# Cross-attention block with a two-expert feed-forward net: weight chunks split from step 8, row ranks in three parts, the first routed tile gathered earlier, two blocks normalised in the setup

## What is computed

```python
def block(x, context, ...):
    x = x + xattn(layernorm(x), context)          # 16 heads of 64, 64 keys
    z = layernorm(x)
    one_hot = argmax(softmax(z @ gate_w.T))       # 2 experts
    masked = z[None] * one_hot.T[:, :, None]      # a row not chosen enters as zeros
    routed = sum_e(relu(masked[e] @ w1[e] + b1[e]) @ w2[e] + b2[e])
    shared = relu(z @ sw1 + sb1) @ sw2 + sb2
    return x + routed + shared                    # hidden size 2048
```

## Time and profile before

| | before |
|---|---|
| time, median of 3 runs | 1908.87 us (1908.34 to 1910.06) |
| the profiled execution | 1907.19 us, span 1905.5 us |
| PE busy | 1826.0 us (96% of the span) |
| DVE, ACT, POOL busy | 798.1, 820.3, 509.2 us |
| mean granted clock of PE | 0.986 of full speed |
| bytes moved | 214.44 MB, mean 113 GB/s |

### The profile page before, as it was taken

The page is one execution under the profiler, slowest core; times in us unless marked ns, Lnnn a source line. Parts: engine busy times, 40 slices in busy tenths (PEclk is TensorE's granted clock), DMA queues, the critical chain, the costliest instruction groups (busy, mean ns, idle before and its releaser), DMA issues.

```text
span 1905.5 us, 33426 instructions
## 1 busy us (share of the span) xinstructions
PE 1826.0 (96%) x11516; PEld 1149.4 (60%) x11517; DVE 798.1 (42%) x1649; ACT 820.3 (43%) x1441; POOL 509.2 (27%) x477
## 2 busy tenths in 40 slices
PE   8979999999799999999999998999999999999997
PEld 6335444544466666666666665666666666666664
DVE  6967778777244433342333333222222222222222
ACT  3645555554333334334444443333333333433333
POOL 2047777776101111221100001122221112122111
PEclk9989999999899999999999999899999999999998
DMA  9235555555942333223344493822121111212100
GB/s 322 83 86 147 161 166 166 175 157 150 267 110 78 100 95 94 90 86 121 121 121 136 151 302 114 247 56 56 51 62 45 38 44 47 60 44 61 51 24 15
DMA packets 230151, 214.44 MB, mean 113 GB/s; under 512 B 130864, under 2 KB 172336, under 8 KB 229680
## 3 DMA queue, kind: packets, MB, share of 16 engines
q1 hardware_dynamic: 221120, 188.09, 34.2%
q0 software_dynamic: 8944, 25.19, 4.3%
HBM read 129.57 MB, written 59.02 MB: 99 GB/s over the span
## 4 chain that ended last, share of the span: by engine, by line
PE 67%; DMA 1%; DVE 1%; issue 1%; ACT 1%; SPq 1%; POOL 0%; POOLq 0%; ACTq 0%
PE pH L998 34%; PE pY L1010 33%; DMA e_split<-s_el 1%; DVE s_el L1341 1%; ACT room_a L1023 0%; ACT s_eh L1255 0%; DVE room_a L1029 0%; SPq L1146 0%; ACT room_a L1021 0%; DMA room_a<-rows_room 0%; SPq L1147 0%; POOL rows_room L1409 0%; DVE room_a L1037 0%; DVE s_work L1296 0%; SPq L980 0%
## 5 line engine op out<-in xcount | busy, mean ns | idle before, releaser
L998 PE MATMUL pH<-room_a,room_w 128*128 128x256 f16 (+1 forms) x6336 | 770.8, 272 | 29.4 <-DMA room_a<-rows_room 10.3
L1010 PE MATMUL pY<-room_w,room_a 128*128 128x512 f16 (+1 forms) x3120 | 755.2, 380 | 6.1 <-DVE room_a L1029 6.1
L998 PEld LDWEIGHTS pH<-room_a,room_w 128*128 (+1 forms) x6336 | 613.1, 98 | 215.6 <-issue 33.3
L1029 DVE TENSOR_TENSOR room_a<-room_a 128x256 f16<-128x256 f32 (+1 forms) x528 | 237.6, 450 | 900.9 <-ACT room_a L1023 900.8
L1010 PEld LDWEIGHTS pY<-room_w,room_a 128*128 128x128 f16 x3120 | 304.7, 98 | 270.0 <-DVE room_a L1029 7.1
L1021 ACT ACTIVATE room_a<-pH,e_bsel,sc 128x256 f32<-128x256 f32 (+1 forms) x272 | 151.7, 558 | 432.9 <-PE pH L998 408.1
L1021 ACT ACTIVATE room_a<-pH,b1s,sc 128x256 f32<-128x256 f32 x256 | 144.1, 563 | 360.1 <-PE pH L998 360.1
L1205 POOL TENSOR_TENSOR room_a<-room_a,s_brow 128x512 f32<-128x512 f32 x32 | 42.4, 1344 | 543.6 <-DVE room_a L1037 543.6
L470 PE MATMUL pO<-room_w,room_b 128*128 (+1 forms) x768 | 172.7, 382 | 4.8 <-DVE room_b L682 4.8
L1023 ACT ACTIVATE room_a<-pH,e_bsel,sc 128x256 f16<-128x256 f32 (+1 forms) x272 | 149.5, 550 | 0.0
L1023 ACT ACTIVATE room_a<-pH,b1s,sc 128x256 f16<-128x256 f32 x256 | 142.4, 556 | 0.0
(11 more groups left out here) (175 smaller groups left out, 1341.7 us busy)
## 6 DMA issues: line engine op xcount, KB each, us to landing
s_er<-in_w SPq DMA_DIRECT2D x64, 512.0 KB, 5.0
room_w<-e_split SPq DMA_DIRECT2D x8, 2048.0 KB, 18.6
rows_room<-in_x SPq DMA_DIRECT2D x32, 256.0 KB, 3.0
room_a<-in_sw SPq DMA_DIRECT2D x32, 256.0 KB, 4.2
room_b<-in_x SPq DMA_DIRECT2D x32, 256.0 KB, 3.7
s_split<-room_a SPq DMA_DIRECT2D x64, 128.0 KB, 3.8
x_scratch<-room_b SPq DMA_DIRECT2D x32, 256.0 KB, 4.0
z_split<-room_b SPq DMA_DIRECT2D x32, 256.0 KB, 4.1
```

Source lines behind the costliest of these rows:

```text
L998: mm = q.matmul(self.pH[j % 2][:, 0:rows], w[:, k, j * P:(j + 1) * P], zt[:, u, k, 0:rows], start=(n == 0), stop=(n == 3 * KC - 1))
L1010: mm = q.matmul(self.pY[u][r][:, :], h[:, j % self.HR, r * P:(r + 1) * P], w[:, j, :], start=(j == 0 and n == 0), stop=(j == HC - 1 and n ...
L1029: q.tensor_tensor(self.hl[:, j % self.HR, 0:rows], self.hf[:, j % self.HR, 0:rows], self.hh[:, j % self.HR, 0:rows], ALU.subtract).then_in ...
```

## The change

1. `AT` becomes `(8, 13)`: the first chunk of each shared tile is handled at steps 8 to 10 and no longer at 10 to 12. This holds for the looking in tiles 0 to 7 as well as for the splitting in tiles 8 to 15.
2. `slots` is cut into `row_ranks` (13 instructions, after step 4 of tile 1), `tile_experts` (8, after step 7) and `row_slots` (9, after step 10).
3. `by_tiles` and the picking of routed tile 0 move from step 13 of tile 15 to step 12 of tile 14; POOL gathers before the bias of tile 14; SP transposes before it stores the last chunk. Result, bias and store of shared tile 15 move behind the barrier, into the experts' block: DVE takes the result after `lo_h` of step 1 of routed tile 0, POOL adds the bias before its first wait, and SP stores it before `load_set`. The bias row `brow` gets a room that lives through both blocks.
4. Row blocks 0 and 1 are both normalised within the setup: DVE's statistics at i = 13 and 16, ACT's `normal` ahead of products `NM + 20` and `NM + 23`, and `lo_x` of both on DVE (at i = 23 and 26) instead of POOL.

```diff
@@ block 1 @@
+                def early(g, u, d):
+                    return isinstance(g, int) and 0 <= N * g + u + d <= 1
...
-                            if n == NF - 5:
-                                normal(act, 0, 0)
+                            if n in (NM + 20, NM + 23):
+                                normal(act, 0, (n - NM - 20) // 3)
...
                         deviation(pool, 0, 0)
+                        deviation(pool, 0, 1)
                         pool.wait_ge(s_max, 3)
                         pool.partition_all_reduce(amsr[:, :], ams[:, :], P, RMAX).then_inc(reduced, 1)
                         pool.memset(least, -NEG).then_inc(S["least_set"], 1)
-                        lo_x(pool, 0, 0)
+                        pool.wait_ge(S["xl"], 2)
...
-                            if i == 15:
-                                stats(dve, 0, 0)
-                                stats_done(dve, 0, 0)
-                                aggregate(dve, 0, 0)
-                                add_eps(dve, 0, 0)
-                                shifts(dve, 0, 0)
+                            if i in (13, 16):
+                                stats(dve, 0, (i - 13) // 3)
+                                stats_done(dve, 0, (i - 13) // 3)
+                                aggregate(dve, 0, (i - 13) // 3)
+                                add_eps(dve, 0, (i - 13) // 3)
+                            if i in (15, 18):
+                                shifts(dve, 0, (i - 15) // 3)
+                            if i in (23, 26):
+                                lo_x(dve, 0, (i - 23) // 3)
@@ blocks 2 and 3 @@
+def add_bias(q, g, u, net, brow):
+    q.wait_ge(net.S["o"], net.tile(g, u) + 1)
+    for r in range(net.R):
+        v = q.tensor_tensor(net.ob[:, u, r, :], net.ob[:, u, r, :], brow[:, :], ALU.add)
+    v.then_inc(net.S["ob"], 1)
+
+def store_rows(sp, net, res_d, t):
+    sp.wait_ge(net.S["ob"], t + 1)
+    sp.dma_start(net.rows(res_d, t), net.ob[:, t % net.N, :, :]).then_inc(net.S["out", t % net.N], 16)
...
-        AT = (10, 13)
+        AT = (8, 13)
...
+                sp.wait_ge(S["h"], HC * (TILES - 1))
+                enet.transpose_rows(sp, 0)
                 store_e(2 * TILES - 1)
-                store(TILES - 1)
-                enet.transpose_rows(sp, 0)
...
-                        step(pool, g, u, -1, bias)
+                        if last_tile(g, u):
+                            gather(pool, enet, enet.zb, z_d, iz, 0, 0, enet.S["pick_z"], "rows_in")
+                        if not past(g, u):
+                            step(pool, g, u, -1, add_bias, net, brow)
...
-                            if j == 3:
+                            if j == 3 and not past(g, u):
                                 step(dve, g, u, -1, net.result, 16, 16)
...
-                            if j == 3 and isinstance(g, int) and g == 0 and u == 1:
-                                slots()
-                            if j == 13 and last_tile(g, u):
+                            if isinstance(g, int) and N * g + u == 1 and j in (4, 7, 10):
+                                {4: row_ranks, 7: tile_experts, 10: row_slots}[j]()
+                            if j == 12 and N * g + u == TILES - 2:
                                 by_tiles()
                                 pick_rows(dve, enet, iz, order, 0, 0, enet.S["pick_z"])
...
             def _(sp):
                 sp.dma_start(b2r[:, :, :].rearrange("p e n -> p (e n)"), b2.rearrange("e n -> (e n)").partition_broadcast(P)).then_inc(S["b2_in"], 16)
+                store_rows(sp, snet, res_d, TILES - 1)
                 sp.wait_ge(snet.S["e_out"], 64 * TILES)
...
+                add_bias(pool, TILES // N - 1, 1, snet, brow)
...
                             step(dve, g, u, 0, net.lo_h, j)
+                            if j == 1 and first_tile(g, u, 0):
+                                snet.result(dve, TILES // N - 1, 1, 16, 16)
```

More of the change, by code:

```diff
@@ L334, in last_tile, with lo_x @@
                     return isinstance(g, int) and N * g + u == SUB - 1
+                def early(g, u, d):
+                    return isinstance(g, int) and 0 <= N * g + u + d <= 1
+                def lo_x(e, g, u):
+                    e.wait_ge(S["xn"], count(g, u))
+                    e.tensor_tensor(xs[:, u % 2, DM:2 * DM], xnf[:, u % 2, :], xs[:, u % 2, 0:DM], ALU.subtract).then_inc(S["xl"], 1)
                 def first_tile(g, u, d):
@@ L584, in body @@
                                 step(act, g, u, -1, normal2)
-                                if not first_tile(g, u, 4):
+                                if not early(g, u, 4):
                                     step(act, g, u, 4, normal)
@@ L1126, in load_r @@
                     sp.dma_start(net.rb[:, t % N, :, :], net.rows(x1_d, t)).then_inc(S["r_in", t % N], 16)
-                def store(t):
-                    sp.wait_ge(S["ob"], t + 1)
-                    sp.dma_start(net.rows(res_d, t), net.ob[:, t % N, :, :]).then_inc(S["out", t % N], 16)
                 def load_e(q):
@@ L1175, in _ @@
                     if t > 0:
-                        store(t - 1)
+                        store_rows(sp, net, res_d, t - 1)
                     if t >= PASS:
@@ L1200, in place_rows @@
                                                 bounds_check=SLOTS - 1, oob_is_err=False).then_inc(S["scattered"], 16)
-                def bias(q, g, u):
-                    q.wait_ge(S["o"], net.tile(g, u) + 1)
-                    for r in range(net.R):
-                        v = q.tensor_tensor(net.ob[:, u, r, :], net.ob[:, u, r, :], brow[:, :], ALU.add)
-                    v.then_inc(S["ob"], 1)
                 def body(g):
@@ L1283, in expert_scales, with row_ranks @@
                     assert steps[0] == EXP_STEPS, steps[0]
-                def slots():
-                    link, steps = linker(dve, S["sort"])
+                link_sort, sorted_steps = linker(dve, S["sort"])
+                before, total, run0, run1, slot = (work[:, n, :] for n in range(5))
+                count1, e0_tiles = run1[:, SUB - 1:SUB], work[:, 5, 0:1]
+                def row_ranks():
+                    link, run, other = link_sort, run0, run1
                     dve.wait_ge(S["ranks"], 1)
-                    before, total, run, other, slot = (work[:, n, :] for n in range(5))
                     link(dve.tensor_copy(before, pR[:, 0:SUB]))
@@ L1298, in slots, with tile_experts @@
                         d *= 2
-                    count1, e0_tiles = run[:, SUB - 1:SUB], work[:, 5, 0:1]
+                def tile_experts():
+                    link = link_sort
                     link(dve.tensor_scalar(is1[:, 0:HALF], starts[:, 0:HALF], count1, float(ROWS), ALU.add, ALU.is_ge))
@@ L1309, in slots, with row_slots @@
                     link(dve.tensor_scalar(half_at[:, :], lane[:, 0:SLOT_SUBS], half_sub, None, ALU.is_equal))
+                def row_slots():
+                    link, run, other = link_sort, run1, run0
                     link(dve.tensor_tensor(other, run, total, ALU.subtract))
@@ L1318, in slots @@
                     link(dve.tensor_copy(worki[:, :], slot))
-                    assert steps[0] == SORT_STEPS, steps[0]
+                    assert sorted_steps[0] == SORT_STEPS, sorted_steps[0]
                 def by_tiles():
```

21 lines of the change are left out of this document (8 added, 13 removed).

## The result

The changed kernel took 1880.2 us (median of 4 runs, 1879.3 to 1881.7), the kernel before 1909.4 (1908.3 to 1910.1): ratio 0.985, 95% interval 0.983 to 0.987, or 26 to 32 us less.

A forecast was written before the change was run, and what follows sets the result against it. PE works 96% of the span, so its stops and the slow matmuls behind them count. Terms 11.0 + 5.5 + 8.0 + 4.5 = 29.0 us off the median gave 1880 us; range 1876 to 1889.

The forecast's parts named there:

- case A: Whole kernel: the terms hold as summed, 1880 us, within small errors 1877 to 1884; chance 0.64.
- three signs of being wrong: `lo_x` several microseconds on DVE; PE waiting for a transfer starting routed tile 1; ACT idling over 3.3 us before second chunk.
- Chunks, 11.0: Shared tiles 8 to 15: with the first chunk at step 8, ACT's wait for stores goes, saving 11.0 us.
- the free 3.3 us: Shared tiles 8 to 15: up to 3.3 us of ACT's wait for a store is not felt by PE.
- Case D: Shared tiles: stores issued at step 10 land as late as before, so the chunks' 11.0 us is lost, 1891; chance 0.06.
- Ranks, 5.5: Shared tile 1: three parts remove PE's 3.7 us stop for `lo_h` and 1.8 us of slow matmuls, saving 5.5 us.
- The border, 8.0: Border of blocks 2 and 3: PE starts 8.0 us earlier, plus 0.8 for fewer slow matmuls, less 0.8 waiting.
- I take 0.8: Start of routed tile 1: the cushion of 12 us is used up, so PE waits 0.8 us.
- case C: Routed tile 1 waits: load and transposes need 4 us more, with 1.8 us of slow matmuls, 1886; chance 0.12.
- Case E: Block 3: the store of shared tile 15's result holds up SP's queue, slower than before, 1922 us; chance 0.03.
- Two blocks in the setup, 4.5: End of the setup: `sim` starts right behind the splits and `masked` comes 4.5 us earlier.
- Case B: Setup: DVE is held in `lo_x` until POOL's reduction is over, gain 23.1 us, 1886; chance 0.11.

The follow-up runs named there:

- r1: The changed kernel with the first chunk back at step 10 (`AT = (10, 13)`), the rest kept: 1895.7 us, ratio 0.9933 to the kernel before.
- r3: The changed kernel with the three parts of the ranks in one piece again, at step 3 of shared tile 1: 1885.6 us, ratio 0.9882 to before.
- e5: The changed kernel with the setup of before (one block normalised there, its low part on POOL): 1887.9 us, ratio 0.9894 to before.
- e7: The changed kernel with the low parts of both blocks on POOL in place of DVE, both still normalised in the setup: 1886.9 us, ratio 0.9884 to before.
- e8: The changed kernel with the store of shared tile 15's result moved behind the load of expert 1's weights in SP's queue: 1879.4 us, ratio 0.9850 to before.
- e9: The changed kernel with chunks at steps 7 and 12, and shared tile 15's result stored behind the weight load: 1877.1 us, ratio 0.9842 to before.
- r4: The changed kernel run again without any edit: 1880.6 us, ratio 0.9855 to the kernel before.
- e10: The changed kernel with chunks back at steps 10 and 13 and the border of before; ranks in parts and setup stay: 1897.3 us, ratio 0.9944 to before.

## Why the prediction was right

The sum of 29.0 us and case A held: 29.2 by the medians. That the two agree within 0.2 us is partly luck. Read from the traces, the terms are 10.3, 5.5, 6.2 and 5.1 to 5.9 us, 27 to 28 in all, with two too large and one too small. Two of the three signs of being wrong that the prediction named did appear, both small: ACT idled more than 3.3 us ahead of one chunk (3.75 in tile 14), and PE waited for a transfer at routed tile 1 (1.7 us).

- **Chunks, 11.0.** At step 15 of tile 15 the first trace is 20.20 us ahead of before (1157.61 and 1177.81), and behind the ranks it was 9.90: 10.3. The mechanism was right (the distance, the free 3.3 us, tile 14 with a stop, though one of only 0.5 us). The step that failed is the separation from the border. Undone alone, this edit costs 15 us and not 11: 2.6 us of that lie behind step 15 of tile 15, where the last store comes 9.2 us behind PE's group and not 6.9, and 3.2 us lie in the longer stop of tile 14. Case D is refuted by the trace, in which six of the seven waits are gone, and by r1, in which they are back.
- **Ranks, 5.5.** Ahead of the ranks' piece PE stood 4.35 us earlier than before, behind it 9.90 (the group of 563.20 is at 553.30 now): 5.55. r3 confirms it.
- **The border, 8.0.** By the trace 6.2: from step 15 of tile 15 to routed tile 1 it took 55.8 us for 61.96. The time of SP's end was exact. Of the 1.8 missing, 0.4 is the time behind SP's end (3.06 for 2.70), 0.4 are slow groups (6.38 us, hardly less than 6.80; I had taken off 0.8), and 0.9 is the wait at routed tile 1 (1.7 for 0.8). That last one was the step "I take 0.8", in which the microsecond of landing had no row either; case C, 4 us more, did not come. Case E did not come either: the issue of the store of the result ended at 1178.5, within routed tile 0.
- **Two blocks in the setup, 4.5.** 5.1 to 5.9 by the traces. `masked` came 6.2 us earlier in the first pair of traces; 0.8 of it was there already when DVE's last pair of splits began (105.27 and 106.03). So the cost of 0.4 for the added work did not show: the splits ended at 106.72, and the forecast was 107.9. And DVE's list behind them took 5.95 us for my 6.4, since L874 took 0.28 us. In the kernel before, the same instruction (L866) took 0.78 us and stood beside POOL's `lo_x` of 106.88 to 108.03:

```profile
107.40 0.78 DVE L866 TENSOR_SCALAR room_a<-room_a 128x256 f32<-128x256 uint8 x1
```

  In e5 POOL's `lo_x` ran from 107.54 to 108.70, and there the instruction behind it was the long one (0.69 us in the changed kernel):

```profile
107.60 1.65 DVE L871 TENSOR_TENSOR pG<-room_a 128x512 f32<-128x512 f32 x1
```

  I had missed that moving `lo_x` off POOL also frees the DVE instructions beside it.
- **Case B is refuted**: each `lo_x` took 0.68 us on DVE, beside or just behind the reduction of 3 columns, and `masked` came early. The Trainium skill ("SBUF — State Buffer", section "Who interferes with whom") says that a DVE instruction with two SBUF inputs contends with a GpSimd instruction that reads SBUF. Where POOL runs a plain two-input operation, the trace agrees: in e7 the DVE instruction L754 took 1.05 us beside POOL's `lo_x`, and the same one 0.22 in the changed kernel (L753). The forecast for case B needed more, namely that the port stays held through the 7 to 8 us in which POOL begins nothing behind the reduction. That did not happen, and the nearer row decided. What POOL does in that time no run shows.

## What to carry to other kernels

Price a distance between two uses of a single buffer by what it takes (here 7.44 us) less the steps between them, and charge PE only with what goes beyond the free part (3.3 us). One step of distance can be worth nearly all of it (10 to 9), and the next one almost nothing (9 to 8). Terms that end in the same wait (the last store here), or whose transfers meet in the same tile (tile 14 here), are not independent: undo them one by one and both together before you trust a term. Cut the stretch in two as well, because a theory of an overlap can give the right time with the overlap in the wrong place. When a queue gets a store that waits for late work, look at what stands behind it: here the load could go ahead of the store at no cost (e8).

## What the runs showed of the hardware

- PE's pace behind a stop. PE's busy time and granted clock in stretches (columns: stretch, us, PE busy and matmuls, granted clock, DMA share, GB/s), first the changed kernel, then e9:

```profile
1163.00:1167.50 4.50, 0.00 (x0) 0.77 0.99 284
1167.50:1174.00 6.50, 6.44 (x38) 0.63 0.13 45
1174.00:1180.00 6.00, 6.00 (x41) 1.00 0.17 59
```

```profile
1165.00:1167.70 2.70, 0.38 (x2) 1.00 0.83 286
1167.70:1172.00 4.30, 4.25 (x37) 1.00 0.92 289
```

  Behind the stop of 4.59 us most of the next 6.5 us ran at 1.2 GHz; behind that of 2.37 us all ran at 2.4 GHz. Between these two traces 2.2 us less of a stop gave 4.4 us: half of the gain was in the matmuls. This is where e9 gained most, and its own forecast had left it out. A stop of 3.05 us was followed by slow matmuls too (r1, tile 14: granted clock 0.59 from 1128.8 to 1133.0).
- The slow stretch is not a fixed price. The 36 matmuls behind the same stop of 4.6 us took 5.53 us (r3), 5.77 (r4), 6.38 (first trace) and 6.82 (e7), full pace being 4.2.
- Without any change of code the stretch from `t_p` to the shared network differed by 3 us between traces (366.4 us in r4, 369.5 in e10), which is as much as some of the terms here.
